# Two cross-attention and expert layers on one core: register tables read in several words, padding cleared earlier, and the second block's rows turned inside the first block

## The chip, the cores and the metric

The kernel runs on one core of one Trainium2 chip. The metric is the device time of one execution in microseconds; a single launch does everything. On the other side of a comparison stands the kernel before, run on the same chip.

## The reference

The input x is (2, 1024, 256), that is 2048 tokens of 256 features; a context of 154 rows per batch feeds two cross attentions. Four steps follow each other, each added to x, each on a layer-normalised x:

```
x = x + L0_xattn(layernorm(x), ctx, mask)     # 16 heads, softmax(QK/4), masked
x = x + L0_ffn(layernorm(x))                  # 8 experts, top 2, silu(x wg) * (x wu) @ wd, inner width 1024
x = x + L1_xattn(layernorm(x), ctx, fside)    # 1 head, additive bias from fside
x = x + L1_ffn(layernorm(x))                  # 8 experts, top 2, gelu(h) * gate @ W2, inner width 512,
                                              # at most 640 tokens per expert
```

In both expert layers the router takes the two largest of 8 logits per token and weighs the two experts' results with a softmax over those two. Which tokens go to which expert is known only at run time.

## The kernel before

Everything is written as one instruction stream per engine, ordered by hand, with semaphores between them (`S("name")`); `wait_ge` of an engine holds all that stands behind it in that engine's stream.

**Expert layers.** Each token's row (256 values as an f16 high part, 256 as a low part, and its token number, gains and first expert) is scattered by GpSimd with indirect DMAs (L690, 32 per layer) into the DRAM table `rows`, which has one region per expert. An expert's tokens are then taken in blocks of 256 rows. The last block of an expert is computed 128 wide if no more are filled. Rows behind the last token of an expert must be zero, so SyncE writes one block of zeros behind each expert's count (`clear_padding`, L436, 8 DMAs of 260 KB at L443); their row numbers depend on the counts.

**The table.** VectorE works out, in `count` (L1815), an int32 table in one SBUF row: words 0 to 8 are the first block of each expert, words 16 on (`TB_ROW`) the row of each block, words 48 to 55 (`TB_PAD`) the row where each expert's padding starts, words 64 to 71 (`TB_FULL`) how many blocks are computed at full width.
**SyncE around the change.** `load_first_block` (L461) waits until enough scatters have landed and loads 256 rows into `x_raw` (L467), raising `xraw` by 16. `clear_padding` waits for table 2 and for `xraw` 16, loads eight words (L441), and issues eight zero DMAs (L443). `load_second_block` (L446) waits for table 3, for VectorE to have taken the first block's shares (`carried`), for TensorE to have turned block 0 (`xbT_ps` 2), loads one word (L451), waits until all scatters and all padding have landed (L453, L454), and loads the second block's rows into the same `x_raw` (L455). In the second layer the weights of expert 2 are asked for behind that (`fetch`, L434).

**TensorE around the change.** `turn_block(g)` (L1034) waits for the rows of block g (`xraw` at 16 g + 16) and transposes them with eight 128x128 matmuls into PSUM bank 6; VectorE copies that to `xbT` (L1928; for block 0 ScalarE, L1383). `one_block` (L1042) computes the gate and up projections (96 matmuls in layer 0, 48 in layer 1) while ScalarE and VectorE make the hidden values and split them into `h_hi` and `h_lo`, and then the output projection in two passes over the hidden chunks: first `h_hi` with both weight parts (32 or 16 matmuls), then `h_lo` with the high weight part (16 or 8 matmuls), into banks 4 and 5. In every block but the first, `turn_block(g + 1)` stands between the up projection and the output projection. Block 0 is written out alone (L1088), without that turn; behind it TensorE waits for table 3, loads eight words of the first part and eight of the `TB_FULL` part one at a time (L1090, L1091), turns block 1 (L1092), and goes into the loop over the experts with those 16 values as loop bounds.

**Others.** VectorE's `first_block` (L1944) ends with weight conversions and `turned(1)`, which copies block 1's `xbT`, takes its shares and raises `carried`. ScalarE's `first_block` (L1380) ends with the eviction of block 0, in layer 1 with the high parts of expert 2's weights (`behind_first`, L1220), and then, once `carried` is 2, with the row load of block 2 (`load(2)`, L1371).

Of the kernel before, what the change touches and what calls it, by code (L numbers as in the profile page):

```python
# [22 lines left out]
P = 128  # L23
# [5 lines left out]
E = 8  # L29
TOP = 2  # L30
N = 2048
NT = N // P
GT = 4
# [8 lines left out]
BLK = 256  # L42
REGION = N + BLK
MAXBLK = N * TOP // BLK + E
AHEAD = MAXBLK + 2
TB_ROW, TB_PAD = 16, 48
TB_FULL = 64
# [26 lines left out]
def two_layers(nc, a, out):  # L74
    with ExitStack() as ctx:
# [5 lines left out]
        def S(name):  # L81
            if name not in sems:
                sems[name] = ctx.enter_context(nc.semaphore(name))
            return sems[name]
# [64 lines left out]
        ctxT, at = part(early, 0, [P, B, KC, SK])  # L149
# [178 lines left out]
        L[0].chunks = [(a[w], 1024 * i, 2048 * n + 1024 * i) for n, w in ((2, "wd"), (0, "wg"), (1, "wu")) for i in range(2)]  # L328
        L[1].chunks = [(a["W1"], 0, 0), (a["W1"], 1024, 1024), (a["W2"], 0, 2048)]

        def wait_counted(eng, sem, value):

            eng.wait_ge(sem, value)
            eng.sem_inc(S("counted"), 1)
# [5 lines left out]
        def _(sp):  # L340
# [95 lines left out]
            def clear_padding(l):  # L436

                sp.wait_ge(S(l.r + "_table"), 2)

                sp.wait_ge(S(l.r + "_xraw"), 16)  # L440
                first = [sp.value_load(table[l.n][0:1, TB_PAD + e:TB_PAD + e + 1], min_val=0, max_val=E * REGION - BLK) for e in range(E)]  # L441
                for row in first:
                    sp.dma_start(rows[bass.ds(row, BLK), :].rearrange("(p s) d -> p (s d)", p=P),  # L443
                                 zeros[:, :]).then_inc(S(l.r + "_padded"), 16)

            def load_second_block(l):  # L446
# [14 lines left out]
            def load_first_block(l):  # L461

                sp.wait_ge(S(l.r + "_table"), 1)
                for n in range(2):
                    sends = sp.value_load(needed[l.n][0:1, n:n + 1], min_val=16 * GT * TOP, max_val=16 * GT * TOP * 2)
                    wait_counted(sp, S(f"{l.r}_scattered{n}"), sends)
                sp.dma_start(x_raw[:, :, :].bitcast(F32), rows[0:BLK, :].rearrange("(h p) d -> p h d", p=P)).then_inc(S(l.r + "_xraw"), 16)  # L467

# [279 lines left out]
        def _(pe):  # L748
            def mm(o, l, r, start, stop, **kw):
                return pe.matmul(o, l, r, start=start, stop=stop, **kw)  # L750
# [278 lines left out]
            def experts(l):  # L1029

                r, tb, pairs = l.r, table[l.n], l.pairs

                def turn_block(g):  # L1034
                    pe.wait_ge(S(r + "_xraw"), g * 16 + 16)
                    for hf in range(2):
                        for part in range(4):
                            last = pe.transpose(psh[:, 6, part * BLK + hf * P:part * BLK + (hf + 1) * P],  # L1038
                                                x_raw[:, hf, part * P:(part + 1) * P], identh[:, :])
                    last.then_inc(S(r + "_xbT_ps"), 1)  # L1040

                def one_block(g, wh, wl, width, turn_next=True):  # L1042

                    pe.wait_ge(S(r + "_xbT"), g + 1)
                    for j in range(pairs):

                        pe.wait_ge(S(r + "_h32"), g * pairs + j + 1)
                        for which, col in enumerate((l.gate_col, l.up_col)):
                            for i in range(2):  # L1050
                                o = ps[:, 2 * (j % 2) + which, i * BLK:i * BLK + width]
                                for kc in range(KC):
                                    at = col(kc, 2 * j + i)
                                    mm(o, wh[:, at:at + P], xbT[:, 0, kc, 0:width], kc == 0, False)
                                    mm(o, wh[:, at:at + P], xbT[:, 1, kc, 0:width], False, False)
                                    last = mm(o, wl[:, at:at + P], xbT[:, 0, kc, 0:width], False, kc == 1)
                            last.then_inc(S(r + "_gu_ps"), 1)
                    if turn_next:
                        turn_block(g + 1)
                    pe.wait_ge(S(r + "_y"), g + 1)  # L1060
                    for c in range(l.hc):
                        if c % 2 == 0:
                            pe.wait_ge(S(r + "_hh"), g * pairs + c // 2 + 1)
                        at = l.down_at + c * D
                        for hf in range(width // P):
                            o, tk = ps[:, 4 + hf, 0:D], slice(hf * P, (hf + 1) * P)
                            mm(o, h_hi[:, c, tk], wh[:, at:at + D], c == 0, False)
                            mm(o, h_hi[:, c, tk], wl[:, at:at + D], False, False)
                    for c in range(l.hc):
                        if c % 2 == 0:  # L1070
                            pe.wait_ge(S(r + "_h"), g * pairs + c // 2 + 3)
                        at = l.down_at + c * D
                        for hf in range(width // P):
                            o, tk = ps[:, 4 + hf, 0:D], slice(hf * P, (hf + 1) * P)
                            last = mm(o, h_lo[:, c, tk], wh[:, at:at + D], False, c == l.hc - 1)
                    last.then_inc(S(r + "_down"), 1)

                pe.sem_inc(S(r + "_xbT_ps"), 1)
                pe.sem_inc(S(r + "_down"), 1)  # L1080
                if l.n == 0:
                    fold_shift()
                route_counts(l)
                turn_block(0)
                pe.wait_ge(S(f"w_ready{l.n}"), len(l.chunks))
                if l.n == 0:
                    pe.wait_ge(S("folded"), 5)
                one_block(0, l.w(0)[:, 0, :], l.w(0)[:, 1, :], BLK, turn_next=False)  # L1088
                pe.wait_ge(S(r + "_table"), 3)
                ends = [0] + [pe.value_load(tb[0:1, e:e + 1], min_val=1, max_val=MAXBLK) for e in range(1, E + 1)]  # L1090
                full_ends = [pe.value_load(tb[0:1, TB_FULL + e:TB_FULL + e + 1], min_val=0, max_val=MAXBLK - 1) for e in range(E)]  # L1091
                turn_block(1)  # L1092
                for e in range(E):
                    first, full_end, end = ends[e] if e else 1, full_ends[e], ends[e + 1]
                    pe.wait_ge(S(f"w_ready{l.n}"), (e + 1) * len(l.chunks))
                    wh, wl = l.w(e % l.slots)[:, 0, :], l.w(e % l.slots)[:, 1, :]
                    with pe.If(full_end - first):
                        with pe.Fori(first, full_end) as g:
                            one_block(g, wh, wl, BLK)
                    with pe.If(end - full_end):  # L1100
                        one_block(full_end, wh, wl, P)
# [1045 lines left out]
```

## Time and profile before

| | us |
|---|---|
| median of 3 runs | 870.74 (870.24 to 872.68) |
| profiled execution, device time | 869.57 |
| its span | 867.8 |
| TensorE busy in the span | 701.9 (81%) |
| VectorE busy | 544.3 (63%) |
| ScalarE busy | 401.6 (46%) |
| GpSimd busy | 333.2 (38%) |
| TensorE's mean granted clock | 0.896 of full |

The profile comes from one execution. Its span runs from the first to the last instruction; the device time is 1.8 us longer. A row of the timeline gives start, length, engine, line, what is written and read, how many instructions were merged, and in brackets how long the engine was idle before and what ended it; "issue" there means that nothing the profile shows was waited for. SPq, ACTq and PEldq are the instruction queues of SyncE, ScalarE and TensorE: register loads, branches and DMA issues stand under these names and are not counted as busy.

### The profile page before, as it was taken

The page shows a single profiled execution, that of the slowest core. Times are in us where ns is not written, and L with a number is a line of the kernel's source. Part 1 is how long each engine was busy: PE and PEld are TensorE (multiplying, and loading weights), DVE is VectorE, ACT ScalarE, POOL GpSimd, SP SyncE. Part 2 cuts the span into 40 slices and gives each one's busy share as a digit, 9 for nine tenths or more (in the row PEclk, how much of TensorE's full clock was granted, in tenths as well). Part 3 has the DMA queues.
Part 4 walks back from the last instruction along what each step waited for, and adds up shares of the span by engine and source line. Part 5 has one row for each costly group of instructions (what it writes and reads, how often), then busy time and mean ns, then how long its engine had stood idle before and what let it go on. Part 6 is the DMA issues. An engine that isn't in the chain of part 4 may idle for free.

```text
span 867.8 us, 18988 instructions
## 1 busy us (share of the span) xinstructions
PE 701.9 (81%) x6280; PEld 553.7 (64%) x6280; DVE 544.3 (63%) x1318; ACT 401.6 (46%) x725; POOL 333.2 (38%) x363
## 2 busy tenths in 40 slices
PE   5676697979788599999998999995860569899991
PEld 4333453646477499998896899985530358677771
DVE  7868576786887345756656747548786345557441
ACT  1234457576746134554645646433453234546331
POOL 7504400355967833131223122322077413434343
PEclk8789799898888799999999999996775779999997
DMA  4563110631447422535536626225032645564332
GB/s 142 106 137 76 44 18 13 172 109 38 149 141 249 129 36 39 170 68 159 152 62 173 172 39 174 42 39 171 25 123 96 206 136 129 133 138 116 60 57 41
DMA packets 68711, 92.83 MB, mean 107 GB/s; under 512 B 14474, under 2 KB 54467, under 8 KB 68636
## 3 DMA queue, kind: packets, MB, share of 16 engines
q1 hardware_dynamic: 43164, 64.97, 25.4%
q0 software_dynamic: 14592, 16.24, 10.7%
q10 hardware_dynamic: 10880, 10.65, 4.7%
q8 instruction: 44, 0.72, 0.4%
q14 instruction: 31, 0.25, 0.1%
HBM read 64.21 MB, written 30.40 MB: 109 GB/s over the span
## 4 chain that ended last, share of the span: by engine, by line
PE 48%; DVE 19%; issue 10%; ACT 8%; DMA 7%; POOL 3%; SPq 2%; ACTq 2%; DVEq 0%; POOLq 0%
PE ps L750 46%; DVE probs L1867 3%; DVE mx L1726 2%; DMA out_x<-keys,row_to 2%; POOL rows L690 1%; ACT probs L1315 1%; DVE keys L1975 1%; PE ps L1038 1%; DMA rows<-zeros 1%; ACT xln L1227 1%; DVE stats L1530 1%; DMA probs<-rows 1%; ACT probs L1419 1%; ACT expo L1312 1%; SPq L441 1%
## 5 line engine op out<-in xcount | busy, mean ns | idle before, releaser
L1975 DVE TENSOR_TENSOR keys<-probs,ps 128x512 f32<-128x512 f32 x116 | 78.8, 687 | 168.0 <-PE ps L750 87.7
L750 PE MATMUL ps<-keys,slot 128*128 128x256 f16 (+1 forms) x1440 | 149.0, 266 | 5.2 <-DVE keys L1928 2.7
L750 PEld LDWEIGHTS ps<-keys,slot 128*128 128x128 f16 x1440 | 129.2, 100 | 23.7 <-issue 7.8
L750 PE MATMUL ps<-keys,probs 128*128 128x256 f16 (+1 forms) x1488 | 139.5, 255 | 5.2 <-DVE probs L1552 3.7
L750 PEld LDWEIGHTS ps<-keys,probs 128*128 128x128 f16 x1488 | 124.2, 98 | 19.1 <-issue 7.2
L630 POOL DMA_INDIRECT attended<-keys,row_to x42 | 66.8, 1591 | 142.1 <-ACT keys L1376 134.6
L1415 ACT ACTIVATE probs<-ps 128x512 f32<-128x512 f32 x116 | 67.8, 598 | 85.7 <-PE ps L750 82.1
L1376 ACT ACTIVATE keys<-ps,carried 128x256 f32<-128x256 f32 x80 | 33.6, 470 | 120.2 <-issue 43.8
L1419 ACT CAST probs<-keys 128x512 f16<-128x512 f32 x116 | 71.1, 614 | 22.0 <-DVE keys L1975 21.9
L1980 DVE TENSOR_TENSOR probs<-keys,probs 128x512 f16<-128x512 f32 x116 | 79.1, 688 | 3.1 <-ACT probs L1419 1.6
L1867 DVE TENSOR_TENSOR probs<-expo,probs 128x512 f16<-128x512 f32 x80 | 59.1, 751 | 32.5 <-ACT probs L1315 32.2
L630 POOL DMA_INDIRECT out_x<-keys,row_to x38 | 59.2, 1558 | 52.3 <-ACT keys L1376 43.4
L750 PE MATMUL ps<-slot,probs 128*128 128x256 f16 x636 | 74.7, 273 | 2.7 <-ACT probs L1419 1.6
L750 PE MATMUL ps<-probs 128*128 128x256 f16 x612 | 71.8, 273 | 3.3 <-ACT probs L1419 2.9
L1312 ACT ACTIVATE expo<-ps 128x512 f32<-128x512 f32 x80 | 48.1, 602 | 49.8 <-PE ps L750 44.0
L750 PEld LDWEIGHTS ps<-slot,probs 128*128 128x128 f16 x636 | 59.9, 98 | 13.7 <-ACT probs L1419 3.3
L750 PEld LDWEIGHTS ps<-probs 128*128 128x128 f16 x612 | 57.5, 98 | 13.7 <-issue 3.2
L626 POOL COPY row_to<-carried 128x2 int32 x40 | 12.0, 299 | 131.2 <-issue 42.9
L1038 PE MATMUL ps<-identh,probs 128*128 128x128 f16 x336 | 26.9, 226 | 30.8 <-issue 18.5
L750 PE MATMUL ps<-penalties,identb 128*128 128x462 bf16 x96 | 35.0, 364 | 17.4 <-DVE mx L1726 7.6
L1315 ACT CAST probs<-expo 128x512 f16<-128x512 f32 x80 | 49.0, 618 | 0.0
L1552 DVE TENSOR_TENSOR probs<-inbox,probs 128x1024 f16<-128x1024 f32 x36 | 43.6, 1232 | 4.0 <-ACT probs L1220 4.0
(296 smaller groups left out, 1185.9 us busy)
## 6 DMA issues: line engine op xcount, KB each, us to landing
inbox<-in_W SPq DMA_DIRECT2D x24, 512.0 KB, 5.1
probs<-rows ACTq DMA_DIRECT2D x40, 260.0 KB, 2.8
inbox<-in_wd SPq DMA_DIRECT2D x16, 512.0 KB, 4.9
inbox<-in_wg SPq DMA_DIRECT2D x16, 512.0 KB, 4.8
inbox<-in_wu SPq DMA_DIRECT2D x16, 512.0 KB, 4.4
rows<-zeros SPq DMA_DIRECT2D x18, 260.0 KB, 3.7
x<-in_x SPq DMA_DIRECT2D x4, 512.0 KB, 6.8
q_out<-queries SPq DMA_DIRECT2D x8, 256.0 KB, 2.1
```

Source lines behind the costliest of these rows:

```text
L630: pool.indirect_dma_start(out=l.sums, out_offset=bass.IndirectOffsetOnAxis(ap=row_to[:, hf:hf + 1], axis=0), in_=yb[:, hf, :], in_offset=N ...
L750: return pe.matmul(o, l, r, start=start, stop=stop, **kw)
L1038: last = pe.transpose(psh[:, 6, part * BLK + hf * P:part * BLK + (hf + 1) * P], x_raw[:, hf, part * P:(part + 1) * P], identh[:, :])
L1312: act.activation(e_ring[:, u % 4, :], ps[:, 4 + u % 2, :], ACT.Exp, scale=float(DK) ** -0.5).then_inc(S("a0_exp"), 1)
L1315: act.copy(p_hi[:, u - 1, :], e_ring[:, (u - 1) % 4, :]).then_inc(S("a0_phi"), 1)
L1376: ins = act.activation(yb[:, hf, :], ps[:, 4 + hf, 0:D], ACT.Identity, scale=carried[:, bass.ds(g, 1), hf, 0:1].rearrange("p b d -> p (b d)"))
L1415: act.activation(s_act[:, j % 2, :], ps[:, 2 * (j % 2), :], l.act).then_inc(S(r + "_s"), 1)
L1419: act.copy(h_hi[:, 2 * j - 2:2 * j, :].rearrange("p c t -> p (c t)"), h32[:, (j - 1) % 2, :]).then_inc(S(r + "_hh"), 1)
L1552: dve.tensor_tensor(w[:, 1, at:at + CH], stage[:, n % STAGES, :], w[:, 0, at:at + CH], ALU.subtract).then_inc(S(f"w_ready{l.n}"), 1)
L1867: dve.tensor_tensor(p_lo[:, u, :], e_ring[:, u % 4, :], p_hi[:, u, :], ALU.subtract).then_inc(S("a0_plo"), 1)
L1975: dve.tensor_tensor(h32[:, j % 2, :], s_act[:, j % 2, :], ps[:, 2 * (j % 2) + 1, :], ALU.mult).then_inc(S(r + "_h32"), 1)
L1980: dve.tensor_tensor(h_lo[:, 2 * j - 2:2 * j, :].rearrange("p c t -> p (c t)"), h32[:, (j - 1) % 2, :], h_hi[:, 2 * j - 2:2 * j, :].rearran ...
```

## The change

Three edits, in both expert layers.

1. `values_at` loads several neighbouring words of the table with one call. SyncE's eight padding words (L441), SyncE's two `needed` words (L465) and TensorE's loop bounds (L1090, L1091) are loaded so. TensorE loads 9 words instead of 8 from the first part, 17 in all instead of 16.
2. In `clear_padding` the wait for the first block's rows (`xraw` 16) moves from ahead of all eight zero DMAs to just ahead of the last one, which is now expert 0's.
3. `turn_block(1)` moves from behind TensorE's register loads into block 0, between the two passes of its output projection.

```diff
+        def values_at(eng, tile, at, n, least, most):
+            return nc.values_load_multi_w_load_instructions(tile[0:1, at:at + n], engines=(eng.engine,), min_val=least, max_val=most)[1]
...
             def clear_padding(l):
 
                 sp.wait_ge(S(l.r + "_table"), 2)
-
-                sp.wait_ge(S(l.r + "_xraw"), 16)
-                first = [sp.value_load(table[l.n][0:1, TB_PAD + e:TB_PAD + e + 1], min_val=0, max_val=E * REGION - BLK) for e in range(E)]
-                for row in first:
-                    sp.dma_start(rows[bass.ds(row, BLK), :].rearrange("(p s) d -> p (s d)", p=P),
+                first = values_at(sp, table[l.n], TB_PAD, E, 0, E * REGION - BLK)
+                for e in (*range(1, E), 0):
+                    if e == 0:
+                        sp.wait_ge(S(l.r + "_xraw"), 16)
+                    sp.dma_start(rows[bass.ds(first[e], BLK), :].rearrange("(p s) d -> p (s d)", p=P),
                                  zeros[:, :]).then_inc(S(l.r + "_padded"), 16)
...
                 sp.wait_ge(S(l.r + "_table"), 1)
-                for n in range(2):
-                    sends = sp.value_load(needed[l.n][0:1, n:n + 1], min_val=16 * GT * TOP, max_val=16 * GT * TOP * 2)
+                for n, sends in enumerate(values_at(sp, needed[l.n], 0, 2, 16 * GT * TOP, 16 * GT * TOP * 2)):
                     wait_counted(sp, S(f"{l.r}_scattered{n}"), sends)
...
-                def one_block(g, wh, wl, width, turn_next=True):
+                def one_block(g, wh, wl, width, first=False):
...
-                    if turn_next:
+                    if not first:
                         turn_block(g + 1)
...
                             mm(o, h_hi[:, c, tk], wh[:, at:at + D], c == 0, False)
                             mm(o, h_hi[:, c, tk], wl[:, at:at + D], False, False)
+                    if first:
+                        turn_block(g + 1)
                     for c in range(l.hc):
...
-                one_block(0, l.w(0)[:, 0, :], l.w(0)[:, 1, :], BLK, turn_next=False)
+                one_block(0, l.w(0)[:, 0, :], l.w(0)[:, 1, :], BLK, first=True)
                 pe.wait_ge(S(r + "_table"), 3)
-                ends = [0] + [pe.value_load(tb[0:1, e:e + 1], min_val=1, max_val=MAXBLK) for e in range(1, E + 1)]
-                full_ends = [pe.value_load(tb[0:1, TB_FULL + e:TB_FULL + e + 1], min_val=0, max_val=MAXBLK - 1) for e in range(E)]
-                turn_block(1)
+                ends = values_at(pe, tb, 0, E + 1, 0, MAXBLK)
+                full_ends = values_at(pe, tb, TB_FULL, E, 0, MAXBLK - 1)
```

## Rows read from the trace of the kernel before

**Rows 1.** The timeline of TensorE's matmuls, layer 0, around block 0.

```profile
268.83 10.64 PE L750 MATMUL ps<-keys,slot 128*128 128x256 f16 x96 [1.31 <-ACT keys L1383]
279.31 5.40 PE L750 MATMUL ps<-slot,probs 128*128 128x256 f16 x48
293.80 1.03 PE L1038 MATMUL ps<-identh,probs 128*128 128x128 f16 x8 [9.09 <-issue]
295.71 12.20 PE L750 MATMUL ps<-keys,slot 128*128 128x256 f16 x96 [0.87 <-DVE keys L1928]
```

**Rows 2.** The same timeline in layer 1.

```profile
686.23 1.92 PE L750 MATMUL ps<-slot,probs 128*128 128x256 f16 x16 [0.41 <-ACT probs L1391]
697.59 1.03 PE L1038 MATMUL ps<-identh,probs 128*128 128x128 f16 x8 [9.44 <-issue]
699.49 8.13 PE L750 MATMUL ps<-keys,slot 128*128 128x256 f16 x48 [0.87 <-DVE keys L1928]
707.46 0.61 PE L1038 MATMUL ps<-identh,probs 128*128 128x128 f16 x8
```

**Rows 3.** Instructions of L1090 and L1091: ns min/median/max, first and last start.

```profile
L1090 PEldq TENSOR_LOAD <-table x8: 298/311/701, 282.6 to 287.5; - x8
...
L1091 PEldq TENSOR_LOAD <-table x8: 295/302/314, 288.6 to 293.2; - x8
...
L1090 PEldq TENSOR_LOAD <-table x8: 297/301/308, 687.0 to 691.5; - x8
```

**Rows 4.** The chain of waits, 296 to 590 us and 700 to 868 us, by line.

```profile
by line: PE ps L750 88.2%; PE ps L1038 2.7%; issue 2.0%; DMA x<-attended 1.4%; DMA inbox<-in_wu 1.4%; DMA attended<-keys,row_to 0.9%; DVE probs L1552 0.8%; DVE probs L1980 0.7%; DVE keys L1975 0.6%; ACT probs L1419 0.4%; ACT probs L1220 0.4
...
by line: PE ps L750 28.7%; issue 19.1%; DMA out_x<-keys,row_to 11.1%; DVE keys L1975 5.0%; ACT probs L1419 4.1%; DVE keys L1928 3.2%; ACT keys L1376 2.7%; ACT probs L1415 2.5%; POOL out_x L630 2.2%; DVE probs L1980 2.2%; ACTq L1370 2.1%; AC
```

**Rows 5.** The chain of waits in layer 0 (start, length, what), and SyncE's zero DMAs.

```profile
267.48 0.27 SPq L441
...
267.79 0.15 SPq L441
...
272.32 5.79 SPq L443 DMA_DIRECT2D rows<-zeros  x8
...
277.15 6.36 DMA rows<-zeros
...
284.07 2.88 DMA probs<-rows
```

**Rows 6.** The same two views in layer 1, and SyncE's weight requests.

```profile
672.23 3.13 DMA probs<-rows
...
680.27 4.56 SPq L443 DMA_DIRECT2D rows<-zeros  x8
...
684.32 3.66 DMA rows<-zeros
...
688.20 2.80 DMA probs<-rows
...
688.94 15.09 SPq L434 DMA_DIRECT2D inbox<-in_W  x6
```

**Rows 7.** The last scatter of each layer; landing times of layer 1's scatters.

```profile
276.83 0.97 POOL L690 DMA_INDIRECT rows<-penalties,slot_s  x1 [0.31 <-issue]
...
679.33 0.97 POOL L690 DMA_INDIRECT rows<-probs,slot_s  x1 [0.30 <-issue]
...
DMA to landing us min/median/max: 2.4/2.5/3.6
```

**Rows 8.** TensorE's granted clock where block 1 begins (column before DMA share).

```profile
294.00:300.00 6.00, 5.13 (x34) 3.83 (x33) 1.22 (x4) 0.60 (x1) 5.19 (x10) 0.59 0.21 57
```

**Rows 9.** VectorE and ScalarE in layer 1; landing of ScalarE's row loads (L1371).

```profile
686.82 3.49 DVE L1552 TENSOR_TENSOR slot<-inbox,slot 128x1024 f16<-128x1024 f32 x3
...
697.30 1.04 ACT L1220 CAST probs<-inbox 128x1024 f16<-128x1024 f32 x1 [0.33 <-DMA inbox<-in_W]
...
DMA to landing us min/median/max: 4.2/4.3/4.3
```

## The prediction

> **What bounds the kernel now.** I read the timeline of TensorE first. Between block 0 and block 1 of each expert layer it stands still: 9.09 us in layer 0 [rows 1], 9.44 us in layer 1 [rows 2], both ended by "issue", so by no semaphore that came late. Next, the instructions of its own queue: they fill just these holes. Eight register loads start at 282.6 and eight more end behind 293.2 in layer 0, and in layer 1 they begin at 687.0 [rows 3]; the turn of block 1 follows at 293.80 and 697.59 [rows 1, 2]. TensorE waits for its own sequencer. The rows of block 1 were not late: they had landed at 286.95 (284.07 + 2.88) and 691.00 [rows 5, 6].
>
> Is TensorE's time the kernel's time afterwards? In layer 0, from 296 to 590 us, 88% of the chain is its matmuls [rows 4], so block 1's start moves everything. In layer 1 it is 29%, with 19% issue and 11% adds of the results by DMA [rows 4]: there it is a round through all engines, but each step follows from the block before it and not from a fixed clock time, apart from the weights at the start (below).
>
> **Part 1: the register loads on TensorE.** One word now costs a TENSOR_LOAD of 0.30 us, then the comparison and the assertion of its bounds. Eight of them start from 288.6 to 293.2, a pitch of 0.66 us [rows 3]; less 0.30 and its gap of about 0.08 this leaves 0.28 us of checks per word. The checks are per value, and I keep them: 17 x 0.28 = 4.8 us. No row shows a TENSOR_LOAD of several words. From below, each of the two costs as much as one word, 2 x 0.30 = 0.6, and L, all loads with checks, is 5.4 us (3.4, if the checks of neighbouring values also merge to half). From above each word is read alone, 17 x 0.30 = 5.1, and L is 9.9. Nothing in the rows leans to either end; I take the middle of the read, 2.8, so L = 7.6 us, against 11.1 (282.6 to 293.7) and 10.6 now.
>
> The Trainium skill speaks against the edit here: "Runtime: NRT & Kernel Launch", section Instruction fetch mechanics, gives a bulk register load about 200 ns per register. By it the read is an estimated 3.4 us and L 8.2, 0.6 us per layer worse than my sum; the trace has only one-word loads, at 300 ns, and can't tell.
>
> **Part 2: SyncE, and when block 1's rows land (T).** Layer 0: the first of eight loads starts at 267.48 with the check 0.31 behind it [rows 5], the zero DMAs start at 272.32, so 0.59 a word, of which 0.27 are checks. After: 8 x 0.25 to 0.27 = 2.1, plus 0.27 to 2.2 for the read, middle 1.2: 3.3 instead of 4.7 us, 1.4 earlier (0.5 to 2.3). The moved wait brings nothing here, since the first block's rows landed before 267. The last zero DMA, issued at 277.15, landed at 283.51 [rows 5]; 1.4 earlier is 282.1. Behind it stands the next wait, the scatters: the last is issued at 276.83, and those of layer 1 land 2.4 to 3.6 us from issue [rows 7], so from 279.3 on; before, both waits were over at 283.5, so that is its latest. Clearing sooner also runs more of it beside the scatters. I take the row load 2.0 us sooner: T = 285.0 (283.7 to 287).
>
> Layer 1: here the moved wait counts. The loads stood behind the landing of block 0's rows, 672.23 + 3.13 = 675.36 [rows 6]; now they stand behind their issue, 672.65. With 3.3 us for loading, the zeros start at 676.0 instead of 680.27, 4.3 sooner, and the last lands 4.3 sooner than 684.32 + 3.66 = 687.98: 683.7. Expert 0's zeros with the moved wait are last, and by then it is long over. The scatters run to 679.33 [rows 7] and land by about 682 to 683; the zeros now run beside them, as in layer 0, where the eight took 11.2 us from first issue to last landing against 7.7 here. So the row load goes out between 682.8 and 687, I take 684.5, and with 2.8 [rows 6] T = 687.3 (686 to 690). The two `needed` words on SyncE are hidden or worth tenths.
>
> **Part 3: the turn inside block 0.** TensorE reaches the point between the passes after 32 of 48 matmuls from 279.31, about 282.9, and after 8 of the 16 matmuls from 686.23, about 687.2 [rows 1, 2]. So the move adds a stall in block 0: T - 282.9 = 2.1 us in layer 0, about none in layer 1. Behind the waiting transposes are queued the `h_lo` pass (1.8 or 0.9 us), the eviction of block 0 on ScalarE and its add on GpSimd; nobody needs these for over 10 us, since block 1's output projection is the next user of the banks. And behind it stand the register loads. Before, they ran while the rows were still on their way and cost nothing until 286.95; now they start only once the rows are there. How far the sequencer runs ahead decides the rest: before it began to load with 2.1 us of matmuls (about 17) still to run in layer 0 (282.6 against the end at 284.7 [rows 1, 3]). So in layer 0 the loads start at T + 0.6 (7 of 24 pairs done), in layer 1, with 16 pairs, at T + 0.1. Branch and first matmul take another 0.5. The copy of the turned rows by VectorE (0.7 us) and its shares lie wholly beside the loads: in layer 1 VectorE is free at 686.82 + 3.49 = 690.3 [rows 9], copy over at 691.0.
>
> Start of block 1's gate and up projection:
> - layer 0: 285.0 + 0.6 + 7.6 + 0.5 = 293.7, against 295.71: **-2.0**
> - layer 1: 687.3 + 0.1 + 7.6 + 0.5 = 695.5, against 699.49: **-4.0**
>
> **The clock.** Where block 1 starts, the granted clock is 0.59 [rows 8], a stretch partly at 1.2 and partly at 2.4 GHz, after 9 us in which TensorE did nothing. The 96 matmuls took 12.20 us against 10.64 in block 0, the 48 of layer 1 8.13, of which (10.64 / 2 = 5.3 at full clock) 2.8 are lost. The hole shrinks to 6 us but doesn't go, so most of the loss stays: **-0.5** for both (0 to -2).
>
> **What is late next in layer 1.** ScalarE converts expert 2's weights ahead of block 2's row load. Their requests start at 688.94 [rows 6]; these need VectorE's conversions from 686.82 on, so they can move up by a microsecond at most, and the last conversion (697.30 + 1.04 [rows 9]) ends at 697.3 to 698.3. A register load and the issue follow (an estimated 0.8 us, from 0.6 a word), and 4.3 us to landing [rows 9]: 702.4 to 703.4. TensorE needs those rows for the turn at 707.46 [rows 2], which with -4 is 703.5. So -4.0 just fits, and about -5 is the most that layer 1 can give.
>
> **Sum.** -2.0 - 4.0 - 0.5 = -6.5 on the profiled execution of 869.57, that is 863.1; it lay 1.2 us under the median of the runs shown, so against 870.74 I forecast **864.2 us**.
>
> **Rivals.**
> - A multi-word load costs like a one-word load (L = 5.4 or less). Layer 0 starts at 291.5 (-4.2), layer 1 at 693.3, but held by the weights to -5; SyncE gains 0.9 more, and 0.5 from the clock: about -10, 860.5. For it: one instruction. Against: the load takes 0.30 us for 4 bytes, so it is all latency, and eight reads may be eight latencies.
> - Each word is read for itself (L = 9.0 to 9.9), rows still earlier: layer 0 at 295.1 to 296 (about -0.2), layer 1 at 697 to 697.8 (-2.1), SyncE's part of T half lost: -2 to -3.5, 868.
> - The lead is eaten later: block 0's add on GpSimd, row loads or weights set the pace and return it. Against: 88% matmuls in layer 0 [rows 4]. For: layer 1's chain. About 870.
> - Slower: rows and register loads no longer overlap. The price is T + 1.1 + L for block 1's start in layer 0, and with L = 9.9 and the row load no sooner (286.95) it is 297.95, 2.2 later than now; in layer 1 (691.0 + 0.6 + 9.9 = 701.5) 2.0 later. It decides as soon as T + L exceeds 294.6 in layer 0 and 698.9 in layer 1; I have 292.6 and 694.9. 875 us. It needs both bad ends.
>
> The skill's rule is a point within the second: L = 8.2 gives -1.4 and -3.4 by the same sum.
>
> **How the numbers follow.** Forecast (862 to 867) 0.50; cheap loads (859.5 to 862) 0.22; word by word (866.5 to 869) 0.16; eaten later (868 to 871) 0.07; slower (873 to 877) 0.05. A measurement can tell 0.3%, 2.6 us, from no change. Faster by more than that, under 868.1: 0.50 + 0.22 + 0.14 = 0.86; within: 0.09; slower 0.05. The range 859.8 to 868.8 leaves out the slower case, most of the absorbed one and the cheapest corner.
>
> **What would show it.** Two TENSOR_LOADs per layer on TensorE's queue instead of 16: their length settles L. The eight transposes of block 1 between matmuls of the output projection, with a stall of about 2 us before them in layer 0 that ends with "DMA probs<-rows", and less than 1 us in layer 1. The hole before block 1: about 6 us, ended by issue. SyncE's zeros in layer 1 from about 676. Block 2's turn in layer 1 near 703. Wrong would be: a stall before the transposes that reaches to 287 or 691; the checks gone or multiplied; or block 1 sooner by 6 us in all and the span not.

## The result, and the profile after

The changed kernel takes 860.63 us (858.22 to 861.59, 4 runs) against 871.71 (870.24 to 874.98, 4 runs) for the kernel before on the same chip: ratio 0.9864, 95% interval 0.9828 to 0.9900. The profiled execution took 861.59 us, its span is 859.9 (867.8 before). Forecast were 864.2 us and faster; the time is in the range, 3.6 us under the forecast, and inside the band of the first rival (859.5 to 862).

The timeline of TensorE around block 0 in layer 0 and layer 1 (start, length, engine, line, what, count, idle before and what ended it); these answer [rows 1, 2]:

```profile
280.29 3.66 PE L752 MATMUL ps<-slot,probs 128*128 128x256 f16 x32
285.93 0.76 PE L1040 MATMUL ps<-identh,probs 128*128 128x128 f16 x8 [1.98 <-DMA probs<-rows]
286.49 3.48 PE L752 MATMUL ps<-slot,probs 128*128 128x256 f16 x16
...
293.55 12.08 PE L752 MATMUL ps<-keys,slot 128*128 128x256 f16 x96 [3.59 <-issue]
...
674.67 7.40 PE L752 MATMUL ps<-keys,slot 128*128 128x256 f16 x48 [1.15 <-issue]
...
683.56 1.05 PE L752 MATMUL ps<-slot,probs 128*128 128x256 f16 x8 [0.42 <-ACT probs L1394]
684.97 0.62 PE L1040 MATMUL ps<-identh,probs 128*128 128x128 f16 x8 [0.36 <-DMA probs<-rows]
685.42 1.04 PE L752 MATMUL ps<-slot,probs 128*128 128x256 f16 x8
692.00 7.28 PE L752 MATMUL ps<-keys,slot 128*128 128x256 f16 x48 [5.54 <-DVE probs L1555]
700.09 0.62 PE L1040 MATMUL ps<-identh,probs 128*128 128x128 f16 x8 [0.81 <-DMA probs<-rows]
```

The transposes (L1040) now stand between the passes. The idle times of 9.09 and 9.44 us have become 1.98 + 3.59 and 0.36 + 5.54. The last one is put down to VectorE's L1555, but that is a conversion of expert 2's weights, of which block 1 uses nothing, and in e5, the same kernel run again, the same hole ends by issue (5.51 us). TensorE's own queue was loading and checking until 691.4, as the next view shows (L332 is `values_at`; ns min/median/max, first and last start; layer 1 alone, then TensorE in both layers, then SyncE in layer 1):

```profile
L332 PEldq FUSED_REGOPS  x17: 146/146/156, 686.0 to 691.2; - x17
...
L332 PEldq TENSOR_LOAD <-table x2: 603/728/852, 685.0 to 688.5; - x2
...
L332 PEldq TENSOR_LOAD <-table x4: 603/732/1049, 286.3 to 688.5; - x4
...
L332 SPq TENSOR_LOAD <-needed x1: 645/645/645, 655.6 to 655.6; - x1
L332 SPq TENSOR_LOAD <-table x1: 531/531/531, 669.8 to 669.8; - x1
```

Two loads per layer instead of 16, but still 17 checks: 9 words in 0.85 us, 8 words in 0.60. From the first load to the last assertion it is 6.4 us in layer 1 (685.0 to 691.4) and 6.6 in layer 0, where the first load took 1.05, against 10.6 and 11.1 [rows 3].

SyncE's queue (timeline, layer 0 then layer 1) answers [rows 5, 6], and its waits in the two stretches:

```profile
271.20 5.54 SPq L446 DMA_DIRECT2D rows<-zeros  x8
283.03 0.42 SPq L458 DMA_DIRECT2D probs<-rows  x1
...
672.54 5.67 SPq L446 DMA_DIRECT2D rows<-zeros  x8
682.31 0.41 SPq L458 DMA_DIRECT2D probs<-rows  x1
685.52 2.60 SPq L437 DMA_DIRECT2D inbox<-in_W  x3
```

```profile
SPq L457 <- DMA rows<-penalties,slot_s: 4.8, 1, 4.8
...
SPq L457 <- DMA rows<-zeros: 2.6, 1, 2.6
```

In layer 0 the row load now waits for the scatters (L457, 4.8 us), no longer for the zeros; in layer 1 still for the zeros.

The granted clock (column before DMA share) of the changed kernel, answering [rows 8]:

```profile
285.00:293.00 8.00, 4.03 (x24) 2.83 (x24) 2.92 (x6) 0.84 (x2) 7.09 (x11) 0.79 0.93 291
293.00:300.00 7.00, 6.45 (x46) 5.24 (x47) 0.69 (x1) 1.48 (x3) 5.99 (x12) 0.76 0.11 39
```

It is 0.76 where block 1 starts, against 0.59; a mix of the levels 2.4 and 1.2 GHz. So the hole is shorter and its price remains in part: 96 matmuls in 12.08 us against 10.64 at full clock.

### The profile page after: what moved, and what is told of

The parts are those of the page before. It is cut to its first block, busy times and chain, and to the rows that moved or that the text cites. A ratio compares the mean times of both kernels' runs of the same rounds, so it can differ in the third digit from the quotient of the medians.

```text
span 859.9 us, 18934 instructions
## 1 busy us (share of the span) xinstructions
PE 700.8 (81%) x6268; PEld 553.7 (64%) x6280; DVE 546.9 (64%) x1318; ACT 401.4 (47%) x725; POOL 332.6 (39%) x363
## 4 chain that ended last, share of the span: by engine, by line
PE 50%; DVE 20%; issue 9%; ACT 8%; DMA 6%; POOL 4%; ACTq 1%; DVEq 0%; POOLq 0%; SPq 0%
PE ps L752 48%; DVE probs L1870 3%; DVE mx L1729 2%; POOL rows L692 2%; DMA out_x<-keys,row_to 2%; ACT probs L1318 1%; DVE keys L1978 1%; ACT xln L1230 1%; PE ps L1040 1%; DVE stats L1533 1%; ACT probs L1422 1%; DVE probs L1983 1%; ACT expo L1315 1%; DVE probs L1555 1%; DVE keys L1931 1%
## 5 line engine op out<-in xcount | busy, mean ns | idle before, releaser
L752 PEld LDWEIGHTS ps<-probs 128*128 128x128 f16 x612 | 57.6, 98 | 13.8 <-issue 3.4
L1555 DVE TENSOR_TENSOR probs<-inbox,probs 128x1024 f16<-128x1024 f32 x36 | 43.8, 1232 | 8.4 <-ACT probs L1223 8.2
L1223 ACT CAST probs<-inbox 128x1024 f16<-128x1024 f32 x36 | 37.2, 1044 | 14.4 <-DMA inbox<-in_wu 10.0
```

The lines of the kernel that those rows point to most:

```text
L1223: act.copy(l.w(slot)[:, 0, at:at + CH], stage[:, n % STAGES, :]).then_inc(S(f"w_hi{l.n}"), 1)
L1555: dve.tensor_tensor(w[:, 1, at:at + CH], stage[:, n % STAGES, :], w[:, 0, at:at + CH], ALU.subtract).then_inc(S(f"w_ready{l.n}"), 1)
```

## The experiments

One measure is read from every timeline: the time from the first gate and up matmul of block 0 to that of block 1 (b1), and from there to that of block 2 (b2). "Layer 0" is the time from block 0's first matmul to the first matmul behind the layer's last block. Ratios are to the kernel before, measured beside each: its median was 871.27 us beside e1 to e4, 870.75 beside e5 to e7 and 872.82 beside e9 and e10.

| kernel | b1, b2 layer 0 | b1, b2 layer 1 | layer 0 | median | ratio (95%) |
|---|---|---|---|---|---|
| before | 26.87, 17.72 | 21.90, 11.32 | 312.1 | 871.71 | |
| changed | 23.74, 17.60 | 17.33, 11.17 | 309.0 | 860.63 | 0.9864 (0.9828 to 0.9900) |
| e5, changed again | 23.22, 17.81 | 16.96, 10.57 | 308.6 | 860.56 | 0.9879 (0.9845 to 0.9913) |
| e1, edit 3 alone | 29.02, 17.93 | 24.76, 9.99 | 314.8 | 875.69 | 1.0054 (1.0029 to 1.0080) |
| e2, edit 1 on TensorE alone | 22.69, 18.06 | 18.22, 14.10 | 308.3 | 863.11 | 0.9893 (0.9852 to 0.9934) |
| e3, SyncE's edits alone | 26.51, 17.81 | 22.35, 11.38 | 312.0 | 868.20 | 0.9971 (0.9943 to 0.9999) |
| e4, all but edit 3 | 22.39, 18.14 | 18.73, 10.58 | 308.2 | 861.68 | 0.9893 (0.9855 to 0.9931) |
| e6, bounds per expert | 17.47, 16.18 | 14.33, 18.34 | 311.1 | 869.84 | 0.9981 (0.9957 to 1.0005) |
| e7, and rows ahead of weights | 17.47, 16.18 | 13.41, 12.47 | 313.0 | 865.81 | 0.9921 (0.9893 to 0.9948) |
| e9, and GpSimd's scaling split | 17.47, 16.18 | 13.07, 14.01 | 303.6 | 855.39 | 0.9809 (0.9776 to 0.9841) |
| e10, e9 with edit 3 | 20.07, 16.17 | 14.44, 15.39 | 304.9 | 857.92 | 0.9848 (0.9805 to 0.9890) |

One warning for the columns of layer 1: b1 there contains block 0's own 48 gate and up matmuls, which no edit touches and which took from 6.76 us (e9) to 8.20 (e4), against 5.41 at full clock. In layer 0 the 96 matmuls of block 0 took 10.64 us in every one of these kernels.

**e1: the turn inside block 0, alone.** The kernel before with

```diff
+                    if first:
+                        turn_block(g + 1)
...
-                turn_block(1)
```

> The kernel before with the turn of block 1 moved between the two passes of block 0's output projection, and nothing else: 16 one-word loads, SyncE as before. Theory (the registers' loads start only once the waiting transposes are through, so rows and loads add up): block 1 starts at 286.95 + 0.6 + 11.1 + 0.5 = 299.2 in layer 0 (295.7 before) and at 691.0 + 0.1 + 10.6 + 0.5 = 702.2 in layer 1 (699.5 before): 6 us slower, about 877. Rival (the moved turn gains by itself, since it leaves the hole): 1 to 3 us faster.

The timeline of TensorE, both layers:

```profile
286.30 0.62 PE L1038 MATMUL ps<-identh,probs 128*128 128x128 f16 x8 [3.00 <-DMA probs<-rows]
...
298.18 2.10 PE L750 MATMUL ps<-keys,slot 128*128 128x256 f16 x9 [9.52 <-issue]
...
694.07 0.81 PE L1038 MATMUL ps<-identh,probs 128*128 128x128 f16 x8 [3.96 <-DMA probs<-rows]
...
705.12 1.25 PE L750 MATMUL ps<-keys,slot 128*128 128x256 f16 x5 [8.54 <-issue]
```

Slower, by 2.2 us in layer 0 and 2.9 in layer 1 to block 1's start, 4.4 in the median (875.69 against 871.27), less than the 6 expected. The wait for the rows (3.00, 3.96 us) is now added ahead of the loads, which filled it before: the mechanism of the fourth rival, here without the other two edits. An instruction that waits holds the register loads behind it.

**e2: TensorE's words alone.** The kernel before with

```diff
+                ends = values_at(pe, tb, 0, E + 1, 0, MAXBLK)
+                full_ends = values_at(pe, tb, TB_FULL, E, 0, MAXBLK - 1)
```

> The kernel before with TensorE's 17 loop bounds loaded in two loads of several words, turn behind them as before, SyncE as before. Theory: loads from 282.6 take 6.6 us instead of 11.1 and end at 289.2, after the rows (286.95); block 1 starts 1.9 us behind, at 291.1, 4.6 us sooner; in layer 1 687.0 + 6.4 + 1.9 = 695.3, 4.2 sooner: 8.8 us in all, as much as the whole change. Rival (the gain needs the turn inside the block): 4 us or less.

```profile
288.62 1.03 PE L1041 MATMUL ps<-identh,probs 128*128 128x128 f16 x8 [4.91 <-issue]
```

Block 1 starts 4.2 and 3.7 us sooner. The last check starts at 288.5 and the turn, right behind, at 288.62: the rows had landed (at 285.61), so the queue is still the bound. This edit alone gives 0.9893, with an interval (0.9852 to 0.9934) that contains the ratio of the whole change and equal to the ratio of e4, where SyncE's edits are added to it: beyond edit 1 on TensorE no gain is shown. In layer 1 of this trace most of the lead is gone at block 2, which starts 32.3 us after block 0 (33.2 before): its rows landed 6.8 us after their issue (692.81 to 699.60), where e4's, issued as far behind block 0, took 5.3 or less and were there in time.

**e3: SyncE's edits alone** (`values_at` on SyncE and the moved wait, both as in the diff of the change).

```diff
+                    if e == 0:
+                        sp.wait_ge(S(l.r + "_xraw"), 16)
```

> The kernel before with SyncE's edits alone (eight padding words and the two needed words in one load each, first seven zero blocks sent before the wait for block 0's rows). TensorE as before. Theory: block 1's rows land 1 to 4 us sooner, but TensorE's loads end when they did, so nothing comes of that; only the needed words, which stand before block 0's row load in layer 1, give 0.6 us: 870 to 871, within 0.3% of before. Rival (the rows were part of the limit): 2 to 5 us faster.

```profile
291.30 1.03 PE L1040 MATMUL ps<-identh,probs 128*128 128x128 f16 x8 [8.73 <-issue]
```

Counted from block 0, the row load of block 1 goes out 2.1 us sooner in layer 0 (13.1 against 15.2) and 2.8 in layer 1 (7.9 against 10.6), and the turn still stands behind 10.7 us of loading (280.5 to 291.2): block 1 moves by -0.4 and +0.5 us. These edits take nothing off the path to block 1 as long as the loads are longer. The ratio's interval just excludes 1, and the median, 3.1 us under that of before, lies where the expectation put its rival; as block 1 did not move, the rows are not the reason, and where the 3 us come from is not shown.

**e4: the changed kernel with the turn put back behind the loads.**

```diff
-                    if first:
-                        turn_block(g + 1)
...
+                turn_block(1)
```

> The changed kernel with the turn of block 1 put back behind TensorE's loads, all loads of several words and SyncE's edits kept. Theory: in layer 0 the loads run while the rows are on their way, and block 1 starts 1.5 us sooner than in the changed kernel; in layer 1 both come to the same within 0.5 us. 9 to 10.5 us faster than before, 0 to 2 us faster than the changed kernel (so a ratio of 0.988 to 0.990). Rival (the moved turn is what pays): 3 to 6 us faster than before only.

```profile
289.33 1.03 PE L1040 MATMUL ps<-identh,probs 128*128 128x128 f16 x8 [4.61 <-issue]
...
688.66 1.03 PE L1040 MATMUL ps<-identh,probs 128*128 128x128 f16 x8 [5.23 <-issue]
```

So what the turn inside does in the changed kernel is the difference to e4: block 1 starts 1.35 us later in layer 0 and 1.40 sooner in layer 1, of which 0.8 are block 0's own matmuls (7.40 us against 8.20). In layer 0 the loads start 16.5 us after block 0 instead of 13.8 (+2.7), in layer 1 at the same 10.4 (0.8 later, less those matmuls); and in both the turn and VectorE's copy no longer stand between loads and block 1 (-1.3: from the last assertion to block 1 it is 1.9 us in e4, 0.6 in the changed kernel). What edit 3 costs in layer 0 it gives back at most in layer 1; in the medians (861.68, 860.56) and ratios (0.9893, 0.9879) it can't be told from nothing.

**e5: the changed kernel again**, without an edit.

> The changed kernel once more, beside the next two on the same chip. 1.0 to 1.4% faster than before; block 1 starts 23.7 us after block 0 in layer 0 and 17.3 us in layer 1, within 0.7 us.

860.56 us, and block 1 starts 0.5 and 0.4 us sooner than in the first measurement.

**e6: each expert's bounds loaded when they are needed.** e4 with two words ahead of the loop, and the next two during each expert:

```diff
+                first, (end, full_end) = 1, bounds_of(0)
+                turn_block(1)
...
+                    after = bounds_of(e + 1) if e + 1 < E else None
```

> SyncE's edits kept, the turn of block 1 behind the loads, and of the 17 loop bounds only expert 0's two are loaded there, one word each with its checks; each later expert's two are loaded before the last, narrow block of the expert ahead, while TensorE has matmuls queued. Theory (the loads cost what of them lies behind the landing of the rows, and two words hide under queued matmuls): in layer 0 block 1 starts as soon as its rows are turned, 18.0 us after block 0 instead of 23.7; in layer 1 12.7 instead of 17.3, but block 2 no more than 1 us sooner than in the kernel with the turn behind, since ScalarE converts expert 2's weights ahead of block 2's row load. About 857, 14 us under before (ratio 0.982 to 0.986). Rival (the loads at each expert's start stall TensorE there, 7 per layer by 1.3 us): 866 or more.

The hole is gone and block 1 starts 9.4 and 7.6 us sooner than in the kernel before, yet the time is that of before. Timelines of TensorE, ScalarE and GpSimd, and the chain from 290 to 320 us by line:

```profile
314.00 7.37 PE L752 MATMUL ps<-keys,slot 128*128 128x256 f16 x48 [6.61 <-DVE keys L1982]
...
701.16 1.04 PE L1040 MATMUL ps<-identh,probs 128*128 128x128 f16 x8 [5.31 <-DMA probs<-rows]
```

```profile
311.73 0.84 ACT L1383 ACTIVATE keys<-ps,carried 128x256 f32<-128x256 f32 x2 [13.89 <-POOLq L637]
```

```profile
302.43 0.51 POOL L650 TENSOR_TENSOR keys<-keys,turned_masks 128x154 f32<-128x154 f32 x1
304.45 0.19 POOL L628 COPY row_to<-carried 128x2 int32 x1 [1.52 <-issue]
305.73 1.66 POOL L632 DMA_INDIRECT attended<-keys,row_to  x1 [1.09 <-issue]
307.69 1.57 POOL L632 DMA_INDIRECT attended<-keys,row_to  x1 [0.30 <-issue]
```

```profile
by line: POOL keys L648 22.3%; PE ps L752 20.2%; issue 17.4%; POOL keys L650 15.3%; DMA attended<-keys,row_to 12.6%; POOLq L624 2.4%; DVE keys L1982 2.3%; ACT probs L1422 2.0%; POOLq L625 1.8%; POOL attended L632 1.1%; POOL row_to L628 0.7%
```

GpSimd scales the next attention's bias (`scale_phi`, 16 tiles, L648 and L650) until 302.9; only then does it add block 0's results (305.7 on). Block 1's eviction on ScalarE (L1383) needs the buffer and stands 13.9 us; what ScalarE owes block 2 comes late, TensorE stands 6.61 us in the middle of block 2 and goes on at a granted clock of 0.73 (48 matmuls in 7.37 us against 5.40). In layer 1 the same lead meets the other half of the prediction's third rival: block 2's turn waits 5.31 us for its rows. The stalls that this run's own rival named are there too, but smaller: ahead of narrow blocks TensorE stands three times in layer 1, 2.5 us in all, and once in layer 0, 0.5 us, each ended by "issue".

**e7: e6 with block 2's row load ahead of expert 2's weight conversions on ScalarE.**

```diff
-                    for n in l.behind_first:
-                        high_part(l, l.early, l.early, n)
...
+                    for n in l.behind_first:
+                        high_part(l, l.early, l.early, n)
```

> The kernel above, and ScalarE sends block 2's row load ahead of the three conversions of expert 2's weights instead of behind them. Theory: in layer 1 the turn of block 2 no longer waits for rows, but the hidden values of block 1 still stand behind the same conversions on ScalarE and VectorE, so 1 to 2 us of the some 4 held there come free: 855 to 856. Rival (the row load alone held it): 4 us, 853. Layer 0 the same within 0.3 us.

4 us faster than e6, the rival's size: that wait falls from 5.31 to 1.58 us. (Block 1's start in layer 1, 0.9 us sooner than in e6, is block 0's own matmuls: 7.11 us against 8.03.) Layer 0 is as in e6, a stall of 6.58 us in block 2 included.

**e8: words read and not used.** The changed kernel with nine further loads between the layers.

```diff
+            for at, n in ((0, 1), (0, 2), (0, 4), (0, 8), (64, 8), (0, 9), (64, 9), (16, 16), (64, 1)):
```

> The changed kernel, and TensorE's queue loads 1, 2, 4, 8 (from word 0), 8 (from word 64), 9 (0), 9 (64), 16 (16) and 1 word without checks where TensorE waits for x between the layers; the values are not used. If a load costs a fixed part and one per word as the 0.30 us of one word and the 0.60 of eight say, then 2 words 0.34, 4 words 0.43, 9 words 0.64, 16 words 0.95. Rival (nine words took 0.85 and 1.05 us because they cross a boundary of 8 words): 9 words 0.85 or more, 16 words 1.1 or more. The span not changed.

Loads whose values nothing uses are not in its trace, so it says nothing of them; as a further run of the changed kernel it took 860.41 us.

**e9: e7 with `scale_phi` in four parts**, one ahead of the adds and one behind those of each of the experts 0, 1 and 2.

```diff
+                for t in range(4 * part, 4 * part + 4):
...
+                for e in range(whole):
+                    add_results(l, e)
+                    scale_phi(e + 1)
...
+            scale_phi(0)
```

> Edit: e7_rows_before_weights, and the 16 tiles of GpSimd's scale_phi are done in four parts, one ahead of the adds of layer 0's results and one behind the adds of each of the experts 0, 1 and 2. Theory (the lead of 6 us in layer 0 was lost because GpSimd was scaling until 303 us of the trace, so block 0's add, block 1's eviction on ScalarE and with it the hidden values of block 2 came late): block 1 still starts 17.5 us after block 0, the stall of 6.6 us at block 2 is gone, blocks 1 and 2 run at full clock, layer 0 takes 301 to 304 us from block 0's start to its end instead of 308.6 in the changed kernel; layer 1 as in e7, 2 to 3 us better than the changed kernel. About 853, ratio 0.980. Rival (another wait returns it: the weights of expert 1, or ScalarE's own pace): a stall of similar size stands at block 2 or 3 with another releaser, 860 or more, ratio 0.988 or above.

The theory held for layer 0, and the time is 855.39 us, 2 us over the expected. The clock of TensorE and its timeline through blocks 1 and 2:

```profile
285.00:293.00 8.00, 6.89 (x64) 6.18 (x65) 3.42 (x8) 2.29 (x6) 4.71 (x5) 1.00 0.78 243
293.00:300.00 7.00, 7.00 (x71) 6.32 (x69) 4.24 (x9) 2.69 (x5) 0.31 (x2) 1.00 0.17 22
```

```profile
284.35 0.61 PE L1046 MATMUL ps<-identh,probs 128*128 128x128 f16 x8
286.11 10.65 PE L758 MATMUL ps<-keys,slot 128*128 128x256 f16 x96 [1.15 <-DVE keys L1941]
...
302.28 10.64 PE L758 MATMUL ps<-keys,slot 128*128 128x256 f16 x96
...
689.46 0.62 PE L1046 MATMUL ps<-identh,probs 128*128 128x128 f16 x8 [2.20 <-DMA probs<-rows]
...
719.65 2.85 PE L758 MATMUL ps<-keys,slot 128*128 128x128 f16 x48 [0.82 <-issue]
```

No stall at block 2 of layer 0, full clock through blocks 1 and 2; block 0's add is issued at 289.58. Layer 0 takes 303.6 us, 5.4 less than in the changed kernel. What is left there is a stall of 4.0 us at 462 us behind a conversion of weights, which stands in the kernel before (3.7) and in the changed one (3.9) too. The median is 10 us under e7 and 5 under the changed kernel; the interval (to 0.9841) ends just under that of e5 (from 0.9845) and overlaps that of the first measurement of the changed kernel (from 0.9828) by a hair.

Layer 1 gives little: block 2 comes 1.4 us sooner than in the changed kernel, but the layer's matmuls end 173.2 us after block 0, against 168.1. Part of this is the price of loading bounds there, where blocks are short: ahead of four narrow blocks TensorE stands 0.8 us each, 3.3 in all, ended by "issue" as in the last row above, and two one-word loads with their checks fill the 1.3 us before each (for that row, from 717.9 to 719.1). The same holes stand in e7 (3.5 us) and in no kernel that loads all bounds at once. e6, e7 and e9 also stand twice for 2.0 us behind conversions of weights, which none of those kernels does; why isn't shown. Nor is the rest explained: e7 has the same code in layer 1 and ends after 170.0 us, and the stretch varied from 168.1 to 177.6 among the kernels that load all bounds at once.

**e10: e9 with edit 3** (the diff of e1).

> Edit: e9_phi_split with turn_block(1) between the two passes of block 0's output projection, as in the changed kernel. With only three or four words left to load on TensorE, theory: the turn inside costs its stall in layer 0 (rows about 15.2 us after block 0's start, the first pass done about 2 us sooner), so block 1 starts 18.3 to 18.8 us after block 0 instead of 17.5, and in layer 1, where the rows come with the point, 0 to 1 us sooner than e9 because VectorE's copy lies beside the second pass. In all within 1 us of e9. Rival (the turn inside was worth its place by itself): 2 us or more faster than e9, because the copy of the turned rows leaves the path in both layers.

Block 1 starts 2.6 and 1.4 us later than in e9 (18.3 to 18.8 us were expected in layer 0, 20.07 measured). In layer 0 it is the stall of the turn, 2.07 us, and a granted clock of 0.57 behind it, so that the `h_lo` pass took 3.27 us against 1.9: with little left to load there is nothing that the early turn could hide. In layer 1 it is not the edit but block 0's own matmuls, 8.13 us against 6.76; in both kernels block 1 then waits for VectorE's copy, which stands behind its conversions of expert 2's weights. The median is 2.5 us over e9, but the intervals overlap: no gain by edit 3 is seen, and a loss isn't shown.

**e11 and e12: what a load of several words costs.** The changed kernel, with loads on TensorE's queue between the layers whose values a condition uses; they lengthen that stretch, so the whole times (866.24 and 877.58 us, one execution each) say nothing. The list of (first word, words) is that of e11, then that of e12.

```diff
+            for at, n in ((0, 1), (0, 2), (0, 4), (1, 8), (64, 8), (16, 16)):
+            for at, n in ((64, 8), (1, 8), (0, 2), (0, 3), (0, 4), (1, 4), (2, 4), (3, 1), (4, 8), (2, 8), (0, 12)):
+                values_at(pe, table[0], at, n, 0, 1 << 20)
```

> Edit: the changed kernel, with further loads of table words on TensorE's queue between the layers, whose values are used in a condition so that they stay: runs of 1, 2, 4, 8, 8 (another part of the table) and 16 words. Theory (a run of 8 words is one transfer, what is left over is loaded by itself): 1 word 0.30 us, 2 and 4 words 0.5 to 0.65, 8 words 0.60, 16 words 1.2, as 9 words took 0.85 to 1.05. Rival (a fixed 0.30 and about 0.04 a word): 2 words 0.34, 4 words 0.42, 8 words 0.60, 16 words 0.9.

> Edit: the changed kernel with loads of table words on TensorE's queue between the layers: (first word, words) = (64, 8), (1, 8), (0, 2), (0, 3), (0, 4), (1, 4), (2, 4), (3, 1), (4, 8), (2, 8), (0, 12). The run before this showed 0.32 us for 1 word, 0.55 for 2, 0.34 for 4, 0.60 for 8 from word 64, 1.11 for 16, but 1.94 for 8 words from word 1. Theory (a transfer of about 0.27 us carries four words if they begin at a multiple of four, and one word otherwise): in the same order 0.60, 1.94, 0.55, 0.82, 0.34, 1.0 to 1.1, 1.0 to 1.1, 0.32, 0.60, 1.3 to 2.0, 0.87. Rival (the place does not matter, the 1.94 was a wait for something else on the queue): 8 words take 0.60 from words 1, 2 and 4 too, and 4 words 0.34 from words 1 and 2.

e11 gave 0.32, 0.55, 0.34, 1.94, 0.60 and 1.11 us: neither theory, since 4 words are cheaper than 2 and eight cost 0.60 or 1.94. The loads of e12 one by one, in the order of its list:

```profile
L332 PEldq TENSOR_LOAD <-table x1: 604/604/604, 578.7 to 578.7; - x1
...
L332 PEldq TENSOR_LOAD <-table x1: 2022/2022/2022, 581.7 to 581.7; - x1
...
L332 PEldq TENSOR_LOAD <-table x1: 557/557/557, 586.1 to 586.1; - x1
...
L332 PEldq TENSOR_LOAD <-table x1: 780/780/780, 587.3 to 587.3; - x1
...
L332 PEldq TENSOR_LOAD <-table x1: 340/340/340, 588.9 to 588.9; - x1
...
L332 PEldq TENSOR_LOAD <-table x1: 1017/1017/1017, 590.5 to 590.5; - x1
...
L332 PEldq TENSOR_LOAD <-table x1: 1002/1002/1002, 592.7 to 592.7; - x1
...
L332 PEldq TENSOR_LOAD <-table x1: 304/304/304, 594.9 to 594.9; - x1
...
L332 PEldq TENSOR_LOAD <-table x1: 599/599/599, 595.6 to 595.6; - x1
...
L332 PEldq TENSOR_LOAD <-table x1: 1935/1935/1935, 598.5 to 598.5; - x1
...
L332 PEldq TENSOR_LOAD <-table x1: 851/851/851, 602.8 to 602.8; - x1
```

Eight words from word 64 or 4 take 0.60 us, from word 1 or 2 1.94 to 2.02; four take 0.34 from word 0 and 1.0 from 1 or 2; two cost two. All fit one rule: if a load begins at a multiple of four, about 0.25 us for each whole four words and as much for each word that is left over; if it begins elsewhere, about 0.25 us for every word. (Eight from word 1 took 2.02, eight times 0.25, although the aligned words 4 to 7 lie among them.) The rival, that the place doesn't matter, falls. Why the place matters no run tells.

## Why the prediction was right, and where its sizes were off

- **TensorE waits for its own queue.** Shown: e2 shortens only the loads and block 1 comes 4.2 and 3.7 us sooner; e3 brings only the rows earlier and it doesn't move.
- **L, 7.6 us forecast, 6.6 and 6.4 measured. This is the mis-sized term.** The checks were right (17 x 0.28 = 4.8; 6.4 - 0.85 - 0.60 leaves 4.9 with gaps). The read was put at 2.8, the middle of bounds 0.6 and 5.1, and took 1.45 in layer 1 and 1.66 in layer 0. The middle was no measurement: the price follows alignment, and the change's three reads of the table start at words 0, 64 and 48 (9, 8 and 8 words), all multiples of four. That L came out within 1.2 us is in part luck: the same 17 words, placed otherwise, would have taken some 4 us by the rule of e12 (an estimate), and L 9. The 200 ns a register that the Trainium skill states ("Runtime: NRT & Kernel Launch", Instruction fetch mechanics) would make an estimated 3.4 us of the read, though that page speaks of registers loaded from HBM, and this table lies in SBUF; here aligned words cost 75 ns each (0.60 / 8), and only single and misplaced ones come near the page, 0.24 to 0.30 (1.94 / 8, and one word). Two slips in the prediction: L = 8.2 isn't a point within the second rival, which begins at L = 9.0; by the same sum it gives -5.3 us, about 865.4, inside the forecast's own band. And with half the checks the lower L is 0.6 + 2.4 = 3.0, not 3.4.
- **SyncE and T.** Rows in layer 0 landed by the turn, 16.1 us after block 0 (285.93 - 269.81) against 18.1 before (286.95 - 268.83): 2.0 sooner, as forecast, and for the reason considered, the scatters being last. In layer 1 10.3 against 13.4: 3.1 sooner, 3.7 forecast. The zeros did start 4.8 sooner, but the last was issued at the end of 5.67 us instead of 4.56 [rows 6] and waited for 2.6 more. Beside them the scatters now run, as the prediction assumed; before, the last scatter came first (679.33 against 680.27). That this makes the zeros slower is likely and not shown.
- **The turn inside.** Stall 1.98 us in layer 0 (forecast 2.1) and 0.36 in layer 1 (none); loads at T + 0.4 and T + 0.1. Then 0.6 us from the last check to block 1.
- **Block 1:** -3.1 us in layer 0 (forecast -2.0), of which 1.0 is L, and -4.6 in layer 1 (-4.0): 1.2 from L less 0.6 from T. The prediction took the changed kernel's order as given and didn't ask for the order without edit 3; e4 shows that the turn could have stayed where it was.
- **The clock:** 12.08 against 12.20 and 7.28 against 8.13 us for block 1's matmuls, -1.0 against -0.5. In layer 1 this is not had, since block 2's turn waits for its rows.
- **Late next in layer 1.** Counted from block 0, block 2's turn was forecast at 24.8 to 25.8 us and stands at 25.4 (700.09 - 674.67), behind a wait of 0.81 for its rows: right. In e6, with block 1 another 3 us sooner, that wait grows to 5.31 and block 2's first matmul stands where it stood before (32.7 us after block 0 against 33.2), as "at most -5" implies.
- **The sum.** The spans differ by 7.9 us, 6.5 forecast: -3.1 in layer 0, -5.0 in layer 1, -0.8 in the attention between, +1.0 ahead of block 0 where nothing was changed. For layer 1 this is one pair of executions: from block 0 to the end of the layer e3, whose first blocks stand as before, took 177.6 us, the kernel before 173.1, the changed one 168.1 and 169.2 (e5). So that the whole 5.0 come from block 1 is not shown by the spans. The medians differ by 10 to 11 us; the last 2 to 3 are that the profiled execution before lay 1.2 under its median and the one after 1.0 over its own. As a ratio the forecast (0.9925) lies outside the interval: the time is in the range, but the gain was underrated, by 1.0 and 1.2 us through L and for the rest by amounts that no single term accounts for.
- **The rivals.** Cheap loads: the time came out there, but L did not (6.6 and 6.4 against 5.4 or less): a read is neither one latency nor eight but two or three. Word by word and the slower case need L near 9.9; e1 is the slower case realised, with L as before (11.1 and 10.6). "Eaten later" didn't happen to a lead of 3 to 5 us; e6 shows that it did to one of 9, through just the engines it named.

## What to carry to other kernels

Register loads on an engine's queue are work of that engine: look for "issue" behind a hole and count them. Place words that are read together at a multiple of four and read them in fours; where the loads still stand in a hole, spreading them over the loop removes it, at 0.8 us for each short block that they don't fit under; and don't put a waiting instruction ahead of loads that could run during the wait, unless what it hides is worth more than the wait. Before shortening one hole further, follow the chain of the shorter version: at 9 us of lead the next bound in layer 0 was GpSimd's side work in front of block 0's add, and only moving that made the lead pay.

## What the runs showed of the hardware that was not expected

- A TENSOR_LOAD costs by aligned groups of four words, as told under e12: 4 words (0.34 us) less than 2 (0.55).
- A bounds check costs 0.28 us per value on TensorE's queue, about what four more aligned words add to a read (0.25). In the changed kernel some 4.8 of its 6.4 us are checks. Leaving them out wasn't tried.
- In e9, with no longer idle time than 1.15 us before block 1's matmuls, the granted clock stayed at 1.00 from 278 to 300 us; in the changed kernel, with holes of 1.98 and 3.59 us, it was 0.79 and 0.76 from 285 on.
